# Experts stage: the second half's routing exponentials on GpSimd, its choice of experts in two pieces

## The reference, cut to what matters

```python
logits = h @ router_w.T                      # 1024 tokens x 16 experts
probs = softmax(logits)
top_vals, top_idx = top_k(probs, 4)
top_vals = top_vals / max(top_vals.sum(-1), 1e-9)
comb = zeros(N, 16).at[arange(N)[:, None], top_idx].add(top_vals)
g, u = einsum('nh,ehi->eni', h, w_gate), einsum('nh,ehi->eni', h, w_up)
routed = einsum('enh,ne->nh', einsum('eni,eih->enh', silu(g) * u, w_down), comb)
shared = silu(h @ sh_gate) * (h @ sh_up) @ sh_down
out = h_in + routed + sigmoid(h @ sh_gate_w) * shared
```

## Time and profile before

| | |
|---|---|
| time, median of 3 runs | 1047.26 us (1047.2 to 1047.94) |
| the profiled execution's own time | 1048.04 us |
| its span | 1046.2 us |
| busy: TensorE | 896.8 us, 86% of the span |
| busy: VectorE | 801.4 us, 77% |
| busy: ScalarE | 672.7 us, 64% |
| busy: GpSimd | 558.8 us, 53% |

### The profile page before, as it was taken

One profiled execution on the slowest core, in us unless ns is written; L12 is line 12 of the kernel. 1 busy time (PEld: TensorE's weight loads), 2 busy tenths in 40 slices (PEclk: granted clock), 3 DMA queues, 4 the chain that ended last, 5 costly groups with the idle time before them and its releaser, 6 DMA issues.

```text
span 1046.2 us, 16036 instructions
## 1 busy us (share of the span) xinstructions
PE 896.8 (86%) x5388; PEld 578.0 (55%) x5388; DVE 801.4 (77%) x1345; ACT 672.7 (64%) x1585; POOL 558.8 (53%) x422
## 2 busy tenths in 40 slices
PE   6898899567566647798988999999999998999998
PEld 3565553234122214566666677777777665655665
DVE  4578879887999997688888777787877666664454
ACT  2556379787766657688887877887767455433222
POOL 3312447262699974587888766767666353410000
PEclk9899899788799987899999999999999999999999
DMA  9831205001122200000000160140001512213221
GB/s 329 341 139 65 98 0 169 21 1 44 40 81 72 68 21 1 1 2 1 1 1 2 41 179 21 49 132 2 1 2 47 177 61 61 71 58 91 71 66 40
DMA packets 38725, 69.77 MB, mean 67 GB/s; under 512 B 5378, under 2 KB 25282, under 8 KB 37108
## 3 DMA queue, kind: packets, MB, share of 16 engines
q1 hardware_dynamic: 38644, 68.75, 20.0%
HBM read 67.56 MB, written 1.18 MB: 66 GB/s over the span
## 4 chain that ended last, share of the span: by engine, by line
PE 30%; POOL 22%; DVE 21%; issue 18%; ACT 5%; DMA 2%; SPq 0%; POOLq 0%; DVEq 0%; ACTq 0%
PE ps L2450 10%; POOL arena L2354 6%; POOL arena L2369 6%; DVE arena L1126 6%; POOL arena L2359 6%; PE ps L2479 5%; DVE ps L1122 4%; PE ps L451 2%; DMA wide<-in_w_down 1%; PE ps L491 1%; PE ps L727 1%; PE ps L729 1%; PE ps L728 1%; PE ps L484 1%; POOL arena L2349 1%
## 5 line engine op out<-in xcount | busy, mean ns | idle before, releaser
L2369 POOL TENSOR_TENSOR arena<-arena 128x4 f32<-128x4 f32 x96 | 98.5, 1027 | 43.5 <-DVE arena L2129 40.9
L2285 ACT ACTIVATE ps<-ps,arena 128x128 f32<-128x128 f32 x256 | 88.5, 355 | 35.2 <-DVE arena L2108 35.2
L2497 DVE TENSOR_TENSOR arena<-ps,arena 128x512 f32<-128x512 f32 (+1 forms) x56 | 38.6, 690 | 86.4 <-ACT ps L2490 86.4
L2450 PE MATMUL ps<-XT,wide 128*128 128x512 f16 (+1 forms) x384 | 92.4, 379 | 0.9 <-DVE arena L2516 0.9
L2490 ACT ACTIVATE ps<-ps,arena 128x512 f32<-128x512 f32 (+1 forms) x56 | 36.9, 659 | 82.1 <-PE ps L2450 82.1
L2277 ACT ACTIVATE arena<-ps,ones 128x512 f32<-128x512 f32 x96 | 68.0, 780 | 28.9 <-PE ps L1978 28.9
L1267 POOL TENSOR_TENSOR arena<-arena 128x1024 f32<-128x1024 f32 x31 | 72.9, 2353 | 21.3 <-DVE arena L1126 19.2
L1971 PE MATMUL ps<-wide,arena 128*128 128x512 f16 x256 | 67.0, 398 | 18.6 <-DVE arena L2096 10.1
L2479 PE MATMUL ps<-wide,arena 128*128 128x256 f16 (+1 forms) x672 | 82.2, 272 | 0.1
L2479 PEld LDWEIGHTS ps<-wide,arena 128*128 128x128 f16 (+3 forms) x672 | 65.4, 98 | 19.9 <-issue 0.8
L2108 DVE TENSOR_REDUCE arena<-ps 128x4 f32<-128x512 f32 x64 | 43.3, 687 | 41.5 <-PE ps L1988 41.3
(11 more groups left out here) (341 smaller groups left out, 2396.2 us busy)
## 6 DMA issues: line engine op xcount, KB each, us to landing
arena<-scan_rows SPq DMA_DIRECT2D x16, 512.0 KB, 3.6
arena<-comb_rows SPq DMA_DIRECT2D x26, 256.0 KB, 3.2
side<-in_wproj SPq DMA_DIRECT2D x4, 1024.0 KB, 5.5
arena<-in_w_down SPq DMA_DIRECT2D x7, 512.0 KB, 3.7
wide<-in_w_down SPq DMA_DIRECT2D x1, 3584.0 KB, 15.7
side<-in_w_gate SPq DMA_DIRECT2D x1, 3520.0 KB, 19.0
side<-in_w_up SPq DMA_DIRECT2D x1, 3520.0 KB, 12.7
wide<-in_w_gate SPq DMA_DIRECT2D x2, 1728.0 KB, 13.6
```

The source lines that it names most:

```text
L2285: last = act.activation(ps[:, 4 + t, i * P:(i + 1) * P], ps[:, 4 + t, i * P:(i + 1) * P], ACT.Exp, bias=mx[:, t, i:i + 1], accum_out=den[: ...
L2369: pool.tensor_tensor(rs[:, j, :], var[:, j, :], minus_half[:, j, :], ALU.pow).then_inc(rs_ready, 1)
L2450: last = pe.matmul(self.ps[0:m, 2 * up + n % 2, :], y[:, c, :], x[:, c, :], start=(t == 0), stop=(t == len(steps) - 1))
```

## The change

The exponentials leave ScalarE. GpSimd computes them as powers of e, in four instructions of 17 values per partition, one behind the weight pieces of each of the steps 11 to 14; a small buffer `euler` of 17 words is filled with e first, and it stands ahead of the weights' buffers in the arena. `route` is cut in two: `route_best` (sum, reciprocals, probabilities, the four largest) stands after step 16's pieces and `route_comb` (the rest) after step 17's. `turn_comb` goes from step 16 to 18, and `take_comb` from step 17 to 19. The first half calls both pieces of `route` in a row as before, and SyncE's list is the same.

```diff
@@ Moe.__init__ @@
         self.comb = a.take([4, E + 1])
+        self.euler = a.take([E + 1])
         self.combT = a.take([4 * S])
@@ Moe @@
+    def power(self, pool, link, h, b):
+        if b == 0:
+            link(pool.memset(self.euler, math.e))
+            pool.wait_ge(self.logit_taken, 4 * h + 4)
+            wait(pool, self.comb_steps, 3 * h - 2)
+        last = pool.tensor_tensor(self.ex[:, b, :], self.euler, self.logit[:, b, :], ALU.pow)
+        if b == 3:
+            last.then_inc(self.exp_ready, 1)
@@ experts, tensor @@
-            if n == 16:
+            if n == 18:
                 moe.turn_comb(pe, 1, SPARE)
@@ experts, vector @@
-            if n == 13:
-                moe.route(dve, link, 1)
+            if n == 16:
+                moe.route_best(dve, link, 1)
             if n == 17:
+                moe.route_comb(dve, link, 1)
+            if n == 19:
                 moe.take_comb(dve, 1, SPARE)
@@ experts, scalar @@
-            if n == 12:
-                moe.exponential(act, 1)
@@ experts, gpsimd @@
+            if 11 <= n < 15:
+                moe.power(pool, link, 1, n - 11)
```

More of the change, by code:

```diff
@@ L1745, in exponential, with route_best @@
         act.activation(self.ex, self.logit, ACT.Exp).then_inc(self.exp_ready, 1)
+    def power(self, pool, link, h, b):
[6 more added lines that the diff above has]
+            last.then_inc(self.exp_ready, 1)
     def route(self, dve, link, h):
+        self.route_best(dve, link, h)
+        self.route_comb(dve, link, h)
+    def route_best(self, dve, link, h):
         dve.wait_ge(self.exp_ready, h + 1)
@@ L1763, in route, with route_comb @@
         link(last)
+    def route_comb(self, dve, link, h):
+        prob = self.prob[:, :, 0:E]
         link(dve.tensor_tensor(self.left[:, :, 0:E], prob, self.left[:, :, 0:E], ALU.subtract))
```

## The result

| | before | after |
|---|---|---|
| time, median of 6 runs each | 1047.23 us | 1051.07 us (1047.52 to 1052.88) |
| ratio, 95% interval | | 1.0032 (1.0016 to 1.0048) |
| the profiled execution's own time, span | 1048.04, 1046.2 | 1047.52, 1045.7 |
| busy: GpSimd | 558.8 us | 570.9 us |
| from gate product 13 to 23 | 42.99 us | 46.04 us |

The account below looks back on a forecast made before the run. TensorE was taken to bound the kernel, its stalls adding to 3.55 us. Terms -3.55 + 0.7 + 1.6 + 2.7 + 0.2 gave +1.65 us on the median 1047.26: 1048.9 us, 80% range 1045.4 to 1051.8.

Parts of the forecast that it names:

- old pauses gone: TensorE's stalls at up products 14 and 15, from table loads with exponentials and from `route`, both vanish: -3.55 us.
- up product 16: TensorE waits for GpSimd's low part of "in" 17, late behind the powers: +0.7 us.
- up product 18: Late `scale` of "down" 8, then `route_best`, delay gating 17 and `low(16)`, so TensorE waits: +1.6 us.
- up product 21: Step 20's loads stand behind the store of `comb`, which waits for the later copy; gating 20 waits: +2.7 us.
- up product 22: The step after up product 21 has two weight pieces, 4.11 us for TensorE's 3.90: +0.2 us.
- A power's length: One GpSimd power of 17 columns takes 3.30 us; wrong if under 2.6 or over 3.6.
- The line through 4 and 9 columns: Powers of 1.03 and 1.90 us in the trace, 0.175 a column and fixed part 0.33, extended to 17 columns: 3.30 us.
- only then comes `route_best`, 2.17 us: On VectorE, `route_best` follows the `scale` of "down" 8 ending at 886.2; gating 17 starts at about 888.35.
- `route_comb`: On VectorE behind step 17's single piece, 1.07 us covered by 1.3 us of free time: costs nothing.
- no change: Outcome between 1045.17 and 1049.35 us, within about 0.2% or 2.1 us: chance 0.54.
- The likeliest case: Powers 3.0 to 3.6 us, loads 3 to 4.5 behind the copy, time 1047 to 1050.8 us: chance 50%.
- dear powers: Rival: GpSimd powers take 4.3 us, growing the waits at up products 16 and 18; sum +5.65, 1052.9 us; chance 13%.

Follow-up runs that it names:

- experiment 2: Changed kernel with the store of `comb` ahead of step 24's loads instead of step 20's: ratio 1.0017 to before, stretch 44.00 us.
- experiment 3: Changed kernel computing only the last of the four powers, SyncE's list as in the change: ratio 1.0018 to before, stretch 44.73 us.
- experiment 7: Changed kernel with one more power of 4 columns ahead of each of the four: ratio 1.0083 to before, stretch 51.21 us.
- experiment 11: Changed kernel with whole powers in steps 11, 13, 15, 17; choice in steps 20 and 21, copy 23, store before step 26's loads: ratio 0.9974 to before.
- experiment 8: Changed kernel without the first power, store ahead of step 24's loads: ratio 0.9996 to before, stretch 41.57 us.
- experiment 4: Changed kernel with half powers in steps 11 to 18; choice in steps 20 and 21, copy 23, store before step 26's loads: ratio 0.9973 to before.
- experiment 5: Changed kernel with exponentials back on ScalarE, no powers, `route` still in two pieces, store ahead of step 24's loads: ratio 1.0004 to before.

## Why the prediction was right where it was, and where it was not

| term | predicted | measured in the stretch |
|---|---|---|
| old pauses gone | -3.55 | -3.55 |
| up product 16 | +0.7 | +0.27 |
| up product 17 | 0 | +0.10 |
| up product 18 | +1.6 | +2.48 |
| clock behind it | not foreseen | +1.67 |
| up product 21 | +2.7 | +1.86 |
| up product 22 | +0.2 | +0.20 |
| sum | +1.65 | +3.03 (46.04 - 42.99 = 3.05) |

- **Where and why TensorE would wait** was right: no pause at 14 and 15, pauses at 16, 18 and 21, and the chains to them (GpSimd's low parts to `scale` to `route_best`; the copy to the store to the loads). Experiments 2 and 3 take away one chain each.
- **A power's length** was right: 3.06 to 3.33 us, mean 3.21, against 3.30. The line through 4 and 9 columns holds at 17, also with an exponent that varies. The estimate by the Trainium skill's GPSIMD Engine Reference (Performance versus the Vector engine, Elementwise; 12 cycles an element for branching code) was 3.0, and in experiments 7 and 11 all four took 3.05 or 3.06. Its other figure, 2.6 cycles for plain elementwise work, does not fit a power.
- **Up product 16** was over-sized by 0.4 since the first power was the shortest and GpSimd's list ended a little earlier. **Up product 17** was not foreseen: its pause of 0.10 goes back to the `scale` that a low part held until 877.70, by which gating 16 came late.
- **Up product 18** was under-sized by 0.9. The step that failed is "only then comes `route_best`, 2.17 us": it took 3.00 (882.34 to 885.34), since its product ran beside a low part; TensorE, less late at up product 16 than forecast, waited 0.3 more, and `route_best` began 0.3 earlier than forecast, which cancel. I had taken the lengths of `scale` and of the products from places where no low part ran.
- **The clock** was missing. I counted a pause at its own length. Experiment 8 shows that with the last 0.69 us of this one 1.67 us of slow products go as well.
- **`route_comb`** was put at nothing, since 1.3 us of VectorE's time cover its 1.07. It took 1.97 (887.60 to 889.57), as its last product ran beside a low part, and gating 18 came 4.23 us behind gating 17 instead of 3.58: 0.65 us that the copy, the store and the loads inherited.
- **Up product 21**: the chain was the forecast one, with the weights there 4.40 us behind the copy's end instead of 4.1. By the stretched products and this its release came 1.4 us later than forecast, but TensorE itself was late by 4.5 there and not by 2.3 (1.67 of it by the clock), so it waited 0.8 less. The loads' price was therefore partly hidden, and the 3.10 of experiment 3 shows it uncovered. The estimate by the Trainium skill's DMA: Bandwidth & Descriptors (Anatomy of one DMA) that I set aside, 2.2 us for a landing, would have been further off: of the three loads behind the store in the profile after, the slowest landed in 3.7 us. Why is not shown.
- **The chances.** 54% stood on no change. The measured +3.4 us lies beyond the bound of 2.1 by which I divided, in the part called slower (34%). The likeliest case had the right terms for the waits, but its sum was +1.65 and the stretch says +3.05. The range reached to 1051.8 for the sake of dear powers, which did not occur; that the time came inside it by the clock and the held products is luck.

## What to carry to other kernels

An engine that is half idle can still have no room at the place where work is moved to: count its instructions per step of the loop that surrounds them, not over the span, and look for the buffer that hands its lateness back. When a producer is moved later, look up what stands behind it in each queue; here one DMA store, left where it was, cost 2 us, and in experiment 3, with TensorE nearly on time, it stood behind a pause of 3.10 and 1.67 of slow products. The same powers spread over seven or eight steps instead of four, with choice, copy and store moved on behind them, turned +3.4 us into -2.8; how much of that each of the two moves gives is an estimate only (experiment 11).

## What the runs showed of the hardware

- **VectorE beside GpSimd's subtraction (`low_part`).** Five instructions of VectorE in the changed kernel (fp32 `scale` from SBUF to SBUF, and products of two SBUF operands) that began during a low part ended with it, 0.7 to 0.9 us late; beside powers `scale` kept its 0.47. The product of 64 columns took 1.06 in experiments 3, 4, 5 and 11 too, and 0.23 in experiment 7, where no low part ran at its start. VectorE's instructions with an operand in PSUM that began beside a low part kept their length in these steps of every profile (`gating` 0.69, `low` 0.68, `weigh` 0.75; before, gating 18 at 889.48 is one). The Trainium skill's GPSIMD Engine Reference (Specifications) names contention with VectorE instructions in a two-port mode or with two SBUF inputs; beside low parts the runs agree for two SBUF inputs and put the price at the rest of the GpSimd instruction; whether `scale` runs in a two-port mode no run shows. Beside powers, 62 `scale` in these steps of all profiles took 0.47 to 0.50; no product with two SBUF inputs ever began beside a power, so this is open for them.
- **The clock behind a pause.** In these steps, behind idle times of TensorE of 1.18 to 1.72 us (the two of before among them) the granted clock stayed at 1.00; behind 2.33, 2.78, 2.94 and 3.08 us it fell to the 1.2 GHz level, and each fall cost 1.67 to 1.69 us. The two pauses of the kernel before (up products late by 1.75 and 1.59, 3.34 in all) were thus cheaper than the one at up product 18 after (2.48 and 1.67, 4.15 in all).
- **Scatter.** The stretch repeats to 0.01 us between profiles of the same kernel (46.04 and 46.04; 39.96 and 39.95), while the spans of these differ by 4 and 1.2 us. What varies lies in the earlier stages, where the mean granted clock differs between these profiles. A question about one stage is better put to its stretch than to the total.
